# A graph network's last stage: chunks normalized in three groups instead of two, and turned over six slots

## The reference

```python
h = maximum(layernorm(x), 0)
x = x + relu(graph_convolution(batchnorm(h @ W.T + b), src, dst))   # first layer
h = maximum(layernorm(x), 0)                                        # "h2" in the kernel
agg = segment_sum(edge_attr, dst)
z1 = relu(concat(h, agg, u) @ W1 + b1)
z2 = relu(z1 @ W2 + b2)
x = x + z2 @ W3 + b3
```

## Time and profile before

| | |
|---|---|
| median of 3 runs | 729.8 us (727.41 to 731.34) |
| profiled execution, time | 722.88 us |
| profiled execution, span | 721.1 us |
| busy share of the span: TensorE, VectorE, ScalarE, GpSimd | 92%, 79%, 63%, 21% |
| mean granted TensorE clock | 0.976 of full speed |
| last stage | 656.3 to 721.1 us |
| one output transfer of 256 KB, issue to landing | 2.3 us |

### The profile page before, as it was taken

How to read it: one execution, slowest core, us unless ns; L and a number is a source line. 1 busy time by engine, 2 the same in 40 slices (tenths; PEclk the granted TensorE clock), 3 DMA queues, 4 the chain that set the end, 5 groups by cost and what they waited for, 6 DMA issues and landing times. The chain is left out here.

```text
span 721.1 us, 21554 instructions
## 1 busy us (share of the span) xinstructions
PE 665.7 (92%) x9010; PEld 571.8 (79%) x9010; DVE 567.3 (79%) x1106; ACT 457.2 (63%) x811; POOL 153.0 (21%) x205
## 2 busy tenths in 40 slices
PE   3986657999999999999999999989999999998997
PEld 2765555888888889888888889978988888896554
DVE  7997988988888888888888886688888889835632
ACT  4563685666667666666666766376666676667863
POOL 8752832110111111110011111010000000013622
PEclk9997697999999999999999999999999999999999
DMA  9002514645455655544444556555444456660122
GB/s 256 19 1 86 194 25 172 228 171 178 175 184 215 218 218 218 215 172 174 171 175 187 216 218 219 207 217 207 176 173 173 178 210 218 218 175 5 43 60 77
DMA packets 64972, 119.75 MB, mean 166 GB/s; under 512 B 3170, under 2 KB 22832, under 8 KB 64900
## 3 DMA queue, kind: packets, MB, share of 16 engines
q1 hardware_dynamic: 63332, 117.82, 46.5%
q0 software_dynamic: 576, 1.12, 0.6%
q10 hardware_dynamic: 1008, 0.07, 0.1%
HBM read 115.81 MB, written 4.03 MB: 166 GB/s over the span
## 5 line engine op out<-in xcount | busy, mean ns | idle before, releaser
L1608 PE MATMUL ps_product<-counts_sb,table_sb 128*128 128x240 f16 (+1 forms) x2646 | 408.4, 261 | 0.0
L1442 ACT CAST counts_sb<-ps_counts 128x588 f16<-128x588 f32 x524 | 336.1, 649 | 100.0 <-PE ps_counts L1598 56.6
L1598 PE MATMUL ps_counts<-key_hot,lo_hot 128*128 128x147 bf16 x2096 | 384.6, 231 | 13.0 <-ACT counts_sb L1442 4.5
L1608 PEld LDWEIGHTS ps_product<-counts_sb,table_sb 128*128 128x128 f16 x2646 | 240.2, 97 | 8.2
L1598 PEld LDWEIGHTS ps_counts<-key_hot,lo_hot 128*128 128x128 bf16 x2096 | 198.1, 98 | 57.8 <-ACT counts_sb L1442 17.9
L902 DVE TENSOR_TENSOR key_hot<-key,iota_key 128x1176 bf16<-128x1176 f16 x262 | 200.8, 766 | 0.0
L898 DVE TENSOR_TENSOR lo_hot<-src_lo,iota_key 128x1024 bf16<-128x1024 f16 x262 | 181.1, 691 | 17.0 <-PE ps_counts L1598 12.6
L1426 POOL TENSOR_SCALAR place_hot<-iota_c,slot_now 128x96 f32<-128x96 f32 x81 | 62.1, 779 | 461.6 <-PE ps_place L1644 452.2
L908 DVE TENSOR_TENSOR attr_hot<-rel,iota_w 128x640 f32<-128x640 int16 x81 | 66.7, 826 | 55.4 <-PE ps_sums L1618 55.4
L1618 PE MATMUL ps_sums<-attr,attr_hot 128*32 128x128 f32 x3240 | 95.5, 276 | 0.0
L1618 PEld LDWEIGHTS ps_sums<-attr,attr_hot 128*32 128x32 f32 x3240 | 88.1, 111 | 4.5 <-issue 4.1
(11 more groups left out here) (295 smaller groups left out, 537.1 us busy)
## 6 DMA issues: line engine op xcount, KB each, us to landing
attr<-in_edge_attr_dram SPq DMA_DIRECT2D x80, 1280.0 KB, 8.2
acc<-in_x_dram SPq DMA_DIRECT2D x4, 768.0 KB, 9.5
attr<-in_x_dram SPq DMA_DIRECT2D x12, 256.0 KB, 5.1
out_dram<-y_ring SPq DMA_DIRECT2D x12, 256.0 KB, 2.3
src_padded<-in_src_dram SPq DMA_DIRECT2D x1, 805.5 KB
attr<-in_edge_attr_dram SPq DMA_DIRECT2D x2, 320.0 KB, 7.8
attr<-in_edge_attr_dram SPq DMA_DIRECT2D x1, 640.0 KB, 3.8
raw_d<-in_dst_dram SPq DMA_DIRECT2D x1, 480.0 KB
```

The source lines that it names most:

```text
L1442: act.copy(counts_sb[s % 2][:].rearrange("p h (n t) -> p h n t", n=WN) [:, :, :, k * QUAD:(k + 1) * QUAD], ps_counts[n % 2][:, :, 0:KEYS]. ...
L1598: ins = pe.matmul(ps_counts[quad % 2][:, c, 0:KEYS], lo_hot[:, held, pair, :, q % 2], key_hot[:, held, pair, :, q % 2], start=True, stop=True)
L1608: ins = pe.matmul(ps_product[side][:, 0:SLOTS] if tiles == TS else product, table_sb[:, h, low, :], counts_sb[side][:, h, :] if tiles == T ...
```

## The change

Chunks 4 to 12 are cut into three groups: 4 to 6, 7 and 8, 9 to 12. Slots 0 to 5 turn chunks (4, 5), (6), (7), (8), (9, 10), (11, 12), where slots 0 to 4 turned (4, 5), (6, 7), (8, 9), (10, 11), (12). The variances of the groups are formed in slots 2, 4 and 6, the roots and shifts in slots 3, 5 and 7. The wait ahead of the normalizing follows the new groups.

```diff
-        GROUPS = [slice(0, LEAD * BC), slice(LEAD * BC, 8 * BC), slice(8 * BC, NB)]
+        GROUPS = [slice(0, LEAD * BC), slice(LEAD * BC, 7 * BC), slice(7 * BC, 9 * BC), slice(9 * BC, NB)]
...
-            TURNED_IN = {0: range(4, 6), 1: range(6, 8), 2: range(8, 10), 3: range(10, 12), 4: range(12, CHUNKS)}
-            MEASURED_IN = {2: 1, 5: 2}
-            NORMAL_IN = {3: 1, 6: 2}
+            TURNED_IN = {0: (4, 5), 1: (6,), 2: (7,), 3: (8,), 4: (9, 10), 5: (11, 12)}
+            MEASURED_IN = {2: 1, 4: 2, 6: 3}
+            NORMAL_IN = {3: 1, 5: 2, 7: 3}
...
-                            act.wait_ge(norm_ok, (c >= LEAD) + (c >= 8))
+                            act.wait_ge(norm_ok, 1 + (c >= 7) + (c >= 9))
```

## The result

The changed kernel took 736.63 us (median of 4 runs, 736.3 to 737.17) against 728.71 us: ratio 1.010, 95% interval [1.0066, 1.0135]. A second comparison, 12 runs against 35 of the kernel before on one chip, gave 735.22 against 730.16: 1.0066 [1.0042, 1.009]. It is slower, by 5 to 8 us. The forecast was 733.6, 3.0 us under the first median, which lies 0.1 us above the upper end of the range.

What follows compares the result with a forecast made beforehand. The last stage was taken as bound by a loop over ScalarE and TensorE. Its terms, -1.0 - 0.5 - 0.5 + 0.8 + 3.1 + 0.45 + 1.5 = +3.8 us, added to 729.8 gave 733.6 us; range 729.0 to 736.5.

Steps and rivals of the forecast that it cites:

- The loop: Last stage: a late slot cycles z1, z2, m2, m1 in 4.27 us, plus 0.11 per turned block; z1 delays paid fully.
- The start, -1.0, -0.5, -0.5: Fewer blocks turned early: z1(0) comes 1.0 us earlier, slots 2 and 3 each get 0.5 us shorter.
- Slot 4, +0.8: Slot 4 turns eight blocks instead of one: 5.15 us against 4.37, before any wait for the root.
- the 3.1 of group 2: Slot 4: GpSimd's three sums hold VectorE's variance, so the root and z1(3) come 3.1 us late; both stalls as forecast: 0.56.
- 3.1 over 3.5: Slot 4 stall: 3.1 us taken; the rival, VectorE held to the end of each GpSimd run, gives 3.5; chance 0.08.
- Slot 5, "+0.45": Slot 5 turns five blocks: 4.82 us against 4.36.
- Slot 6, the +1.5 of group 3: x3(2) queues behind GpSimd's sums, delaying y(2), group 3's variance and root: z1(5) at 689.8 instead of 688.3 us.
- Sum: All terms of the last stage together: +3.8 us, giving 733.6 us, 0.5% slower.
- From slot 7 nothing differs: Slots from 7 on stay as in the kernel before, in steps of 4.26 to 4.27 us.
- "Neither root waits", -0.8: Rival: the stalls of groups 2 and 3 both vanish, -0.8 us, 729.0 us; chance 0.07.

Runs made afterwards that it cites:

- the filler: Changed kernel plus three matmuls without use in slot 5, where TensorE stood waiting: ratio 1.0053 [1.003, 1.0077], last stage 68.8 us.

## Why the prediction was right, and where it wasn't

- *The loop.* Slots of 4.27 us plus 0.11 a turned block, z1 paying every delay: right, to 0.1 us, in the slots without a stall (4.13, 4.70, 5.14, 4.81, 4.26).
- *The start, -1.0, -0.5, -0.5.* Measured -1.00, -0.51, -0.49.
- *Slot 4, +0.8 and the 3.1 of group 2.* Together 3.9 forecast, 3.89 measured. The three sums caught three instructions one by one, not at the end of the run as L592 once was the earlier trace rows. Which instructions were caught was off: L857, L859 and L862, not L858, L860 and L862; since each sum caught one, the end came out the same. The choice of 3.1 over 3.5 stood on less than the prediction says: in the earlier trace rows L589 ends (39.18 us) before the first memset starts (39.91), so that row doesn't show it let in between them. L859, with a single tensor input, was held for 1.13 us too. The Trainium skill's page "SBUF — State Buffer", section "Who interferes with whom", names tensor_scalar among the operations that can take the ports shared with GpSimd, when their operands meet conditions. The trace agrees with that: 1.13 us beside a sum, 0.17 in the run where GpSimd waits.
- *Slot 5, "+0.45", is the step that failed.* It measured +2.1 (and +0.44 with the clock held up). I had worked out that z1(3) comes 3.1 us late, which is a TensorE standing for over 3 us, and then costed the slot behind it at the clock of before. The term that is missing is 1.65 us of half clock, shown by the filler. In the kernel before TensorE's longest wait in this stage is 1.35 us, and no row of that stretch shows the clock fall. The Trainium skill's page "TensorE: Matmul & The Clock Gate", section "HAM oscillation", warns of this kind of loss: a pause between matmuls takes the clock to half, and the work behind it pays. The trace agrees, with 0.52 behind 3.22 us of standing. I didn't weigh it; a slower rival, with the clock at half behind the pause, belonged in the forecast.
- *Slot 6, the +1.5 of group 3.* Right at full clock (5.78 us, 1.5 above a free slot), and 1.1 or 0.2 in the changed kernel: the slow m1 had already made z1(4) late, in slot 5, while the sums of group 3 went on.
- *Sum.* +3.8 forecast; +3.8 with the clock held up; +5.0 and +4.2 in two profiles, where the clock takes 1.65 in slot 5 and gives back 0.4 or 1.3 in slot 6. So the half clock costs 1.2 or 0.4 us net. "From slot 7 nothing differs" held. The 3.0 us between the forecast and the first median understate the miss, since the forecast was added to 729.8 and the kernel before measured 728.71 in its four runs. The rest of the 7.9 us between the first medians isn't in the stage: the second comparison gives 5.1, and the start of the stage moves by 8.5 us between executions of one kernel.
- *"Neither root waits", -0.8.* It didn't come by itself, but moving the roots of groups 2 and 3 gave it: -0.7.

## What to carry to other kernels

An instruction that waits should stand behind the work that doesn't need it: the same roots at the end of their slots made 4 to 5 us of loss in the stage into 0.7 us of gain (one profile; the whole kernel showed no difference from before), without touching the groups or the turning. When a forecast contains a stall of TensorE like the 3.2 us here, cost the work behind it at the lower clock as well, and look at what that slowness hides. The 1.35 us of the kernel before brought no fall, and the last stages traced here hold none of a length between the two. Small VectorE instructions in a dependent chain can each be held by a different long GpSimd instruction, so a 0.8 us chain is worth keeping out of a dense run of them.

## What the hardware showed that I had not expected

- TensorE stood for 3.2 us at the same place in both profiles of the changed kernel; the half clock began with the first matmul in one and 1.0 us behind it in the other, and filled stretches of 3.5 and 3.3 us. What sets the moment stays open; it wasn't tried.
- That moment changed the total by 0.9 us (70.1 and 69.2 us), with nothing else different.
- The two executions of the kernel before came apart early: GpSimd's third L1426 starts at 140.06 us in one and at 148.53 in the other, 8.5 us apart, as much as at L1769. The clock is low there for stretches, and not in one direction: 0.57 and 0.68 from 60 to 80 us, 0.91 and 0.67 from 80 to 100. That the clock is the cause is only argued.
- Adding 2.7 us of useless matmuls made a stage 0.4 to 1.3 us shorter.
